# Decoder block: an unrolled load-and-split stage, pipelined projection and context stages, and the second attention's values and sums in one stretch of wide matmuls

## The reference

```
# cross attention, per sequence; 16 heads of size 8
q, k, v = x @ wq + bq, ctx @ wk + bk, ctx @ wv + bv
p = softmax(q @ k.T / sqrt(8))          # 64 x 64 per head
x = x + concat_heads(p @ v) @ wo + bo

# context MLP, per sequence
x = x + gelu_tanh(x @ ctx.T) @ ctx
```

## Time and profile before

| | us |
|---|---|
| three runs | 2485.16, 2493.59, 2495.51 (median 2493.59) |
| the profiled execution | 2487.64, its span 2485.9 |
| granted clock, mean over the span | 0.90 |
| PE, DVE, ACT, POOL busy | 2215.4, 1468.2, 1091.5, 559.9 |
| start to the first attention's first matmul | 44.90 |
| second attention: context turned from 460.1, per-tile loop from 513.87, last add ends at | 737.41 |
| context MLP: context turned from 2214.13, last add ends at | 2253.00 |

### The profile page before, as it was taken

The page is one execution under the profiler, slowest core; times in us unless marked ns, Lnnn a source line. Parts: engine busy times, 40 slices in busy tenths (PEclk is TensorE's granted clock), DMA queues, the critical chain, the costliest instruction groups (busy, mean ns, idle before and its releaser), DMA issues. The chain is left out here.

```text
span 2485.9 us, 95498 instructions
## 1 busy us (share of the span) xinstructions
PE 2215.4 (89%) x42219; PEld 1631.8 (66%) x42219; DVE 1468.2 (59%) x3213; ACT 1091.5 (44%) x1901; POOL 559.9 (23%) x582
## 2 busy tenths in 40 slices
PE   4999998689997679788999989999899997987998
PEld 2566666478873568127888878878788885455545
DVE  6888786345547754685666656666566665354213
ACT  0233334344447775674444435444344443243324
POOL 3656554011103100402222212212122222000100
PEclk7999999766568999888999989999899998986898
DMA  3000000000000000100000000000000001002001
GB/s 87 2 3 2 2 2 2 5 1 0 0 1 13 0 1 1 29 1 3 4 5 4 4 4 4 4 4 4 4 4 4 4 4 49 1 0 68 1 0 34
DMA packets 28107, 22.89 MB, mean 9 GB/s; under 512 B 11705, under 2 KB 22657, under 8 KB 27746
## 3 DMA queue, kind: packets, MB, share of 16 engines
q1 hardware_dynamic: 27298, 17.24, 2.6%
q0 software_dynamic: 448, 0.14, 0.1%
HBM read 15.28 MB, written 2.10 MB: 7 GB/s over the span
## 5 line engine op out<-in xcount | busy, mean ns | idle before, releaser
L1790 PE MATMUL psum<-dr_kq,dr_kSq 64*64 64x64 f32 x6144 | 226.5, 226 | 24.0 <-issue 18.5
L1790 PEld LDWEIGHTS psum<-dr_kq,dr_kSq 64*64 64x64 f32 x6144 | 206.0, 140 | 58.0 <-issue 54.6
L2207 POOL TENSOR_TENSOR dr_kSq<-dr_kSq,dr_decay 128x256 f32<-128x256 f32 x128 | 111.6, 872 | 443.7 <-PE psum L1790 443.7
L1796 PE MATMUL psum<-dr_G,dr_CT 64*64 64x32 f32 x5120 | 189.1, 224 | 1.0 <-issue 1.0
L2119 ACT ACTIVATE dr_Y<-psum 128x256 f32<-128x256 f32 x160 | 63.1, 394 | 284.2 <-PE psum L1796 284.2
L1790 PE MATMUL psum<-dr_GT,dr_Y 64*64 64x32 f32 x5120 | 184.3, 221 | 3.1 <-issue 3.1
L1790 PEld LDWEIGHTS psum<-dr_GT,dr_Y 64*64 64x64 f32 x5120 | 166.5, 136 | 11.1 <-issue 7.4
L1796 PEld LDWEIGHTS psum<-dr_G,dr_CT 64*64 64x64 f32 x5120 | 171.3, 137 | 1.1 <-issue 1.1
L1796 PE MATMUL psum<-dr_Y,dr_GT 64*64 64x32 f32 x4096 | 149.6, 222 | 18.8 <-issue 18.8
L1796 PEld LDWEIGHTS psum<-dr_Y,dr_GT 64*64 64x64 f32 x4096 | 134.1, 136 | 47.4 <-issue 41.3
L2362 DVE TENSOR_TENSOR dr_CT<-psum,dr_minus_masks 128x256 f32<-128x256 f32 x192 | 77.9, 419 | 100.7 <-PE psum L1790 100.7
(11 more groups left out here) (407 smaller groups left out, 5733.5 us busy)
## 6 DMA issues: line engine op xcount, KB each, us to landing
topk_w<-in_L_ffn_w_dram SPq DMA_DIRECT2D x16, 256.0 KB, 5.4
out_dram<-store_rows SPq DMA_DIRECT2D x4, 512.0 KB, 3.6
dout_w<-in_L_attn_Wff_dram SPq DMA_DIRECT2D x3, 256.0 KB, 3.2
attn_w_rows<-in_L_attn_Wq_dram SPq DMA_DIRECT2D x1, 256.0 KB, 3.2
attn_w_rows<-in_L_attn_Wk_dram SPq DMA_DIRECT2D x1, 256.0 KB, 4.0
attn_w_rows<-in_L_attn_Wv_dram SPq DMA_DIRECT2D x1, 256.0 KB, 5.2
attn_w_rows<-in_L_attn_Wo_dram SPq DMA_DIRECT2D x1, 256.0 KB, 6.0
moe_w<-in_L_ffn_w_dram SPq DMA_DIRECT2D x1, 256.0 KB, 3.4
```

Source lines behind the costliest of these rows:

```text
L1790: last = nc.tensor.matmul(out(r), lhsT(r), rhs(r), start=True, stop=True)
L1796: last = nc.tensor.matmul(out(HALVES[1 - j]), lhsT(r), rhs(r), start=True, stop=True)
L2207: pool.tensor_tensor(ks, ks, total.unsqueeze(2).to_broadcast([P, HB * (LR >> l), 1 << l]), ALU.mult).then_inc(kS_scaled[l], 1)
```

## The change

Four things are edited.

1. `load_tokens` is removed. `attention_weights` loads x in four parts, then the weights, the 14 small loads and the context, all on SP. PE turns x as the parts land, DVE copies each group and makes parts two and three per group, ACT casts the first part and copies the turned weights, POOL does the first subtraction.
2. The projections of the second attention become one stage, unrolled over 8 groups: weights and biases are issued together, the context is turned two groups ahead, and q, k and v have semaphores and pairs of banks of their own.
3. The context MLP becomes one unrolled stage: context turned one group ahead, no staging copies of `X` and of the context rows.
4. The second attention's tile: values and sums of all four head groups are made in one stretch behind the output product of the tile behind. The weights are now 32 columns of v (4 heads of 8) or a block of ones, the moving operand is 256 columns of probabilities. The sums come out spread over the rows, are inverted on ACT as exp(-ln(sum)), and multiplied on DVE into `mixed`, which stands already turned; the output product takes four matmuls, each with a copy of wo masked for one head slot. The two halves share one transpose bank. The staging of q and v moves from ACT to POOL.

```diff
     with Stage(k, "attn_w") as t:
+        x_rows = t.sb("x_rows", [P, NT, D])
...
         def _(sync):
+            x = k.a["x"].rearrange("(n u) t d -> (u t) n d", u=2)
+            for c in range(4):
+                sync.dma_start(x_rows[:, c * XC:(c + 1) * XC, :], x[:, c * XC:(c + 1) * XC, :]).then_inc(x_loaded[c], 16)
...
-                pool.dma_start(w.rope_k[:, :, :], k.a["rope_k"]).then_inc(small_loaded, 16)
+                sync.dma_start(w.rope_k[:, :, :], k.a["rope_k"]).then_inc(small_loaded, 16)
+            sync.dma_start(k.ctx_rows[:, :, :],
+                           k.a["ctx_1024"].rearrange("(n u) t d -> (u t) n d", u=2)).then_inc(k.ctx_loaded, 16)
...
+            for g in range(NG):
+                pool.wait_ge(first_part, g + 1)
+                if g >= 3:
+                    pool.wait_ge(second_left, g - 2)
+                pool.tensor_tensor(first[g % 3][:, :], group(k.X, g), group(w.parts[:, 0, :], g), ALU.subtract
+                                   ).then_inc(first_left, 1)
...
+        @block.scalar
+        def _(act):
+            for g in range(NG):
+                act.wait_ge(x_kept, g + 1)
+                act.activation(group(w.parts[:, 0, :], g), group(k.X, g), ACT.Copy).then_inc(first_part, 1)
+            for n, (plain, rot) in enumerate(((w.q, w.q_rot), (w.k, w.k_rot), (w.v, None), (w.o, None))):
+                act.wait_ge(turned, n + 1)
...
+            for i in range(NG + 3):
+                if i < NG:
+                    keep(i)
+                if 2 <= i < NG + 2:
+                    split(i - 2)
+                if i >= 3:
+                    split_rest(i - 3)
...
+                pe.wait_ge(w_kept, 1)
                 pe.wait_ge(bias_loaded, 64)
...
+                for g in range(NG):
+                    if g == 1:
+                        pe.wait_ge(ob_ready, 1)
+                    project(g)
+                    if g < NG - 2:
+                        turn_ctx(g + 2)
...
         def pe_turn(pe, t, c):
             pe.wait_ge(exp_ready[c], t + 1)
+            if c == 1:
+                pe.wait_ge(probsT_ready[0], t + 1)
+            elif later(t, 1):
+                pe.wait_ge(probsT_ready[1], t)
...
+        def pe_values(pe, t, u):
             k.hold(pe)
+            pe.wait_ge(probsT_ready[0], t + 1)
+            pe.wait_ge(probsT_ready[1], t + 1)
+            pe.wait_ge(v_staged, t + 1)
+            if later(t, 1):
+                pe.wait_ge(mixed_kept, t)
+            for at, weights in ((slice(0, W), lambda r, g: v_t[u][r, 32 * g:32 * g + 32]),
+                                (slice(W, 2 * W), lambda r, g: ones[r, :])):
+                for g in range(2 * GH):
+                    for b in range(2):
+                        r = slice(b * T, (b + 1) * T)
+                        last = nc.tensor.matmul(k.psum[32 * g:32 * g + 32, 5 + b, at], weights(r, g),
+                                                probsT[g // GH][r, g % GH, :], start=True, stop=True)
+            last.then_inc(mixed_ready, 1)
...
+        def pe_out(pe, t):
             pe.wait_ge(mixed_kept, t + 1)
             pe.wait_ge(added, t + 1)
+            for n in range(4):
+                last = nc.tensor.matmul(OUT_BANK, wo[:, n, :], mixed[:, n, :, :].rearrange("p b t -> p (b t)"),
+                                        start=(n == 0), stop=(n == 3))
+            last.then_inc(out_ready, 1)
...
             if this:
                 pe_turn(pe, t, 0)
-                pe_turn(pe, t, 1)
             if ahead:
                 pe_scores(pe, t + 1, 1 - u)
-            if behind:
-                pe_turn_mixed(pe, t - 1)
             if this:
-                pe_values(pe, t, u, 0)
-                pe_values(pe, t, u, 1)
+                pe_turn(pe, t, 1)
             if behind:
                 pe_out(pe, t - 1)
+            if this:
+                pe_values(pe, t, u)
...
         def dve_mixed(dve, t):
-            dve.wait_ge(mixed_ready, t + 1)
-            dve.reciprocal(inv[:, :], V_BANK[:, :, XK]).then_inc(inv_ready, 1)
...
+            dve.wait_ge(inverse_ready, t + 1)
+            if later(t, 1):
+                dve.wait_ge(out_ready, t)
+            by_slot = lambda ap: ap.rearrange("p b (n t) -> p b n t", t=T)
+            dve.tensor_tensor(mixed[:, :, :, :].rearrange("p n b t -> p b n t"), by_slot(inverse[:, :, :]), by_slot(SUM),
                               ALU.mult).then_inc(mixed_kept, 1)
...
+        def act_invert(act, t):
+            act.wait_ge(mixed_ready, t + 1)
+            if later(t, 1):
+                act.wait_ge(mixed_kept, t)
+            act.activation(log_total[:, :, :], TOTAL, ACT.Ln).then_inc(log_ready, 1)
+            act.wait_ge(log_ready, t + 1)
+            act.activation(inverse[:, :, :], log_total[:, :, :], ACT.Exp, scale=-1.0).then_inc(inverse_ready, 1)
...
+        def act_step(act, t, u, this=True, ahead=True, behind=True):
+            if behind:
+                act_invert(act, t - 1)
             if this:
                 act_keep(act, t, 0)
                 act_keep(act, t, 1)
-            if behind:
-                act.wait_ge(mixed_turned, t)
-                act.activation(mixedT[:, :], k.bank[7][:, 0:TT], ACT.Copy).then_inc(mixedT_ready, 1)
             if ahead:
                 act_exp(act, t + 1, 0)
                 act_exp(act, t + 1, 1)
-            if this and two_ahead:
-                act_q(act, t + 2, u)
-            if this and ahead:
-                act_v(act, t + 1, 1 - u)
...
     with Stage(k, "cmlp") as s:
-        turn_context(k, s, "cmlp_ctx", 2)
...
+            pe.wait_ge(k.ctx_loaded, 32)
+            turn_ctx(0)
+            for g in range(NG):
+                if g < NG - 1:
+                    turn_ctx(g + 1)
+                hidden(g)
+                if g >= 1:
+                    output(g - 1)
+            output(NG - 1)
...
-        load_tokens(k)
```

More of the change, by code:

```diff
@@ L73, in block @@
         return self.stack.enter_context(self.nc.Block())
[L76 to L114, removed]
@@ L117, in turn_context @@
[L117 to L137, removed]
@@ L271, in _ @@
         @block.tensor
         def _(pe):
+            pe.wait_ge(k.eye_made, 2)
+            for g in range(NG):
+                if g % 2 == 0:
+                    pe.wait_ge(x_loaded[g // 2], 16)
+                for j in range(4):
+                    last = nc.tensor.transpose(k.bank[g][:, j * D:(j + 1) * D], x_rows[:, 4 * g + j, :], k.eye[:, :])
+                last.then_inc(x_turned, 1)
             pe.wait_ge(rows_loaded, 64)
@@ L301, in _, with keep @@
[L301 to L309 removed]
+            def keep(g):
+                dve.wait_ge(x_turned, g + 1)
+                dve.tensor_copy(group(k.X, g), k.bank[g][:, :]).then_inc(x_kept, 1)
@@ new lines, in _ @@
+                pe.wait_ge(k.ctx_loaded, 16)
+                turn_ctx(0)
+                turn_ctx(1)
+                pe.wait_ge(w_loaded, 64)
+                for i in range(4):
+                    last = nc.tensor.transpose(v_bank[1][:, i * D:(i + 1) * D], w_rows[:, i, :], k.eye[:, :])
+                last.then_inc(w_turned, 1)
+                pe.wait_ge(w_kept, 1)
+                pe.wait_ge(bias_loaded, 64)
+                nc.tensor.matmul(v_bank[1][:, 0:1], wT[:, 3, :], bias[:, 2:3], start=True, stop=True).then_inc(wobv_ready, 1)
@@ L917, in _ @@
             pool_spread(pool, 0, 0)
+            pool_v(pool, 0, 0)
             pool_spread(pool, 1, 1)
@@ new lines, in hidden @@
+            def hidden(g):
+                pe.wait_ge(ctx_kept, g + 1)
+                if g >= 2:
+                    pe.wait_ge(gelu_ready, g - 1)
+                for n in range(H):
+                    for half in range(2):
+                        c = (2 * n + half) * T
+                        last = nc.tensor.matmul(h_bank[g % 2][half * T:half * T + T, n * T:(n + 1) * T],
+                                                ctx_g[g % 2][:, c:c + T], k.X[:, g * G + c:g * G + c + T],
+                                                start=True, stop=True)
+                last.then_inc(h_ready, 1)
@@ new lines, in output @@
+            def output(g):
+                pe.wait_ge(gelu_ready, g + 1)
+                if g >= 2:
+                    pe.wait_ge(added, g - 1)
+                for n in range(H):
+                    for half in range(2):
+                        r = slice(half * T, half * T + T)
+                        last = nc.tensor.matmul(y_bank[2 * (g % 2) + half][:, n * T:(n + 1) * T],
+                                                k.ctx_rows[r, H * g + n, :], hid[g % 2][r, n, :], start=True, stop=True)
+                last.then_inc(y_ready, 1)
```

339 lines of the change are left out of this document (165 added, 174 removed).

## The result

| | before | after |
|---|---|---|
| median of the runs | 2489.38 us | 2408.19 us |
| lowest to highest of four runs each | 2483.97 to 2495.51 | 2402.56 to 2413.53 |
| profiled execution, its span | 2487.64, 2485.9 | 2413.53, 2411.8 |
| granted clock, mean of the span | 0.90 | 0.935 |

The account below looks back on a forecast made before the run. The second attention was taken as bound by PE, mostly at the low clock, with PE idle before landings at stage heads. Gains 14 + 17 + 37 + 6.5 = 74.5 from 2487.64 give 2413, forecast 2414; 8-in-10 range 2388 to 2444.

Parts of the forecast that it names:

- A: Kernel start, load and split of x: first attention begins at 30.5 instead of 44.90 us, a gain of 14, bounds 10 and 17.
- B: Projections of the second attention: loads issued together, PE sets the pace, scores begin at about 496.8, gain 17, bounds 14 and 19.
- C: Second attention's tile loop: mostly full clock with drops, about 5.6 us a tile, 186 instead of 223.5, a gain of 37.
- Eight-way overlap of the 64x32 blocks: Values and sums in the second attention: 32 instructions overlap eightfold, 1.7 us at half clock, 0.85 at full.
- The ring: Second attention's tile at full clock: DVE product, four DVE instructions, second exponential, Ln, Exp, next product; about 5.4 us.
- first rival: Clock full throughout the second attention and higher in the context MLP: 5.4 us a tile, 2393 us in all; chance 0.16.
- PE's 6.7 at half clock: Second attention's tile: PE's step of transposes, scores, output, values and sums, and switches costs 6.7 us at half clock.
- D: Context MLP: 32.4 us instead of 38.9 at half clock, a gain of 6.5; at full clock some 19 us, gain 20.
- Same code, no change: Code outside the edited stages: the same, so nothing was counted for it.
- second: Rival: clock stays at half in the second attention, 6.7 us a tile, gain there 3, 2447 us in all; chance 0.10.
- third rival: Second attention's 64x32 blocks overlap only two-way at half clock: 11.8 us a tile, 2605 us in all, slower; chance 0.03.
- fourth: Rival: kernel start and projections gain little, 2 and 5 us instead of 31, landings or ACT's copies late: 2438; chance 0.07.

## Why the prediction was right

**A, 9.7 instead of 14: the step that was mis-sized is DVE's pace.** The casts were put at 0.31, a quarter of the 2048-column row. Alone they take 0.42, and beside POOL's subtraction 1.38. So a group takes 2.96 and not about 2.0, and ACT's last cast, reckoned for about 18.5, ends at 24.80. ACT's copies were cheaper than reckoned (5.6 from 24.80 to 30.41, against 6.5 to 7.5). The rest held: narrow matmuls 3.55, then 1.1. The lower bound of 10, which 9.7 just misses, named this case, with POOL's subtraction as the slow one (it took 1.33, for a reckoned 1.27); it was DVE's cast that paid, and the run with the subtraction on DVE shows it. That run regains only 1.5 of the 4.3 missing, because DVE then has the subtraction itself. The Trainium skill's page "SBUF — State Buffer", section "Who interferes with whom", has a cast in a two-port mode and a GpSimd instruction exclude each other for a whole instruction. By that rule, the trace agrees: the cast issued at 25.11 ended at 26.49, 0.29 behind the end of POOL's subtraction at 26.20. That the small loads would be hidden held; SP issued the last at 18.36.

**B, 17.6 for 17.** As argued: weights and biases land together, idle times of 2.42 and 0.79 in place of 5.41 and 4.84.

**C, 46.8 instead of 37: right in its mechanism, wrong in the clock's drops.** Eight-way overlap of the 64x32 blocks held: 32 instructions take 0.86 to their successor, the 0.85 reckoned. The ring held, with the second exponential directly ahead of Ln: 5.24, not 5.4. What failed is "drops in the ring's idle part, about 5.6 a tile": there were none between 497 and 650, although PE stood idle 23% of it. The term that was mis-sized is the tile's 5.6, at 31 tiles 11 us too much; filling and draining took 14.3 instead of 12.5 and gave 2 back. For this half the first rival was closer, with 43.5. PE's 6.7 at half clock, with 0.3 for switches that no row prices, was not put to the test, since the clock was full in the middle of the loop. The explanation has to be sharpened too. The prediction took the tile from 6.98 to the ring's pace; the runs with added matmuls show the old tile at 4.66 wherever the clock was full. The change didn't shorten the tile, it let the clock stay up. Against the page "TensorE: Matmul & The Clock Gate" of the Trainium skill, whose section "What's actually happening" sets the clock by how busy PE has been, the runs stand as the trace of before did: of three stretches busy 98.29, 98.33 and 100.00 of 100 the clock was 0.63, 1.00 and 0.93, and one busy 77% had 1.00.

**D, 6.4 for 6.5, as one of two outcomes.** At half clock the sum was right. The first rival's price at full clock (19 us) was seen as well, 20.25 in the doubled-values kernel, in the same code. Which one a run gets is not settled by the code of the stage alone: six traced executions ran this same code, four at half clock throughout and two, at 20.25 and 19.99, mostly at full. What decides between them stays open. So that D came out at 6.4 is in part luck, and the prediction gave the other outcome too little chance.

**Same code, no change:** it was not nothing. The delta rule took 979.0 to 996.4 in the profiled runs, at a clock of 0.94 to 0.96, a wider spread than the 11 us between the four runs of the kernel after. So the right total owes something to luck: 6 us too much from the parts, 6 us back from elsewhere in the one profiled execution. By the medians the gain is 81.2, close to the 80.5 of the parts, and the forecast of 2414 is 6 too high.

The second and third rival fell by the clock and by the overlap. The fourth had A at 2 and B at 5, which came at 9.7 and 17.6.

## What to carry to other kernels

Before pricing a stage by its instructions, ask at which of the two clocks each version will run: here a factor of up to two lay in the same instructions, and PE's busy share did not tell which. Adding an unread wide matmul to a stretch of narrow ones is a cheap test of whether clock or work is the price. When a tile is bound by a ring through several queues, write out the second-longest ring before reordering, because moving one link produced a ring of 5.7 in one case and of 5.16 in the other. And work given to POOL was not free for DVE here, where both read and wrote SBUF.

## What was not expected of the hardware

- Work added to a full PE made the kernel faster, by 10 us in the medians with one matmul per tile and with two; the loops were 194.0 us with one (in the fastest run of ten), 205.9 with two, 223.5 with none.
- PE busy 97% of 32.49 us kept the low clock throughout, PE busy 98% of 100 us in the first attention had the full one, and so had PE busy 77% of 153 us.
- The same stage had two outcomes in different runs, 32.49 us at 0.50 and 20.25 at 0.92; in the second the clock fell at the start and came back by itself.
- A 512-column cast of DVE took 1.38 us beside a POOL subtraction and 0.42 alone.
